# A front stage rewritten: convolution split three to one between VectorE and TensorE, softplus and u on VectorE, row clearing moved into the first expert

## The chip, the cores and the metric

The kernel runs on one core of one Trainium2 chip. The metric is the device time of one execution in microseconds, as the median of several runs; lower is better. Beside the runs there is one profiled execution, from whose trace every duration below is read.

The engines are called PE (TensorE), DVE (VectorE), ACT (ScalarE), POOL (GpSimd) and SP (SyncE, which here only issues DMAs). Each works through its own program in order and waits for others by semaphores.

## The reference, cut to what matters

The input x has 2 x 2048 tokens of 512 channels. It is normalised per token; a selective state-space layer and a mixture of eight experts both read the result.

```python
xn = layernorm(x)                                # 4096 tokens, 512 channels
# state-space branch
xc     = causal_conv4(xn, conv_w) + conv_b       # per channel, 4 taps
x_conv = silu(xc)
proj   = x_conv @ xproj_w.T                      # 128 (dt) + 16 (B) + 16 (C)
delta  = softplus(dt_in @ dtproj_w.T + dtproj_b)
a      = exp(delta * A);  b = delta * B_in * x_conv     # 16 states per channel
h      = scan(a * h + b);  s = sum(h * C_in) + xn * D_param
# expert branch: softmax over 8 experts, best 2 of a token, capacity 1024 rows an expert
scores = softmax(xn @ wg);  gate, idx = top_k(scores, 2)
pos    = cumsum(one_hot(idx)) ...                # row of the token in its expert
y      = sum(gate * (gelu(disp @ fc1_w + fc1_b) @ fc2_w + fc2_b)[idx, pos])
out    = x + s * silu(y)
```

## The kernel before

The program has two stages, `front` and `main_loop`, one behind the other with a barrier between them. `main_loop` runs eight experts; beside expert e it does the 16 scans of time chunk e. Each expert is four quarters. `front` prepares what it needs, for eight chunks of 512 tokens (`NCH` = 8, `CH` = 512), each as four blocks of 128 channels (`KT` = 4). `front` is where nearly all of the change lies.

**Normalising (L491 to L520).** Per chunk DVE measures (four `bn_stats`, `bn_aggr`, the addition of EPS), POOL copies the mean and takes the power -1/2 (L445, L447), and DVE then normalises (L512). x arrives in two buffers in turn, `got` and `s_acc` (L175); the normalised rows go to DRAM (L180). PE turns each chunk (L242) so that channels lie on partitions, ACT copies it into `xnT` (L341, L343), PE multiplies by the gate weights (L250) and ACT copies these logits twice (L349, L353). On PE the order is logits of chunk ch, turning of chunk ch+1, turning of the logits of ch.

**Routing (L564 to L614).** A chain of small dependent operations on DVE over all 4096 tokens. It needs one Exp of ACT (L368). Behind the masks PE counts with two matrices, for both choices at once (L276 to L281, into both banks of `pC`). DVE then works out the slot of each choice, and `placed` is raised when both are done. Between the counting and L288 PE waits for `placed`, since `pC` is also where it convolves.

**Convolution to softplus (L283 onwards), a loop over chunks.** Two of the four channel blocks are convolved by DVE (one `tensor_scalar` L539 and three `scalar_tensor_tensor` L543 for each), two by PE as products with diagonal matrices (L288, four taps for each block, in float32, which the trace shows as two matmuls for each product). ACT applies Silu (L376, L380). PE projects (L299, L300), turns the C rows (L316) and widens dt (L309). ACT copies the projection (L387, L390), adds the bias (L404) and does Abs, Exp and Ln (L406, L408, L415), each of Exp, Ln and Silu with a load of its table. Softplus is finished by a correction in five passes: rounding on DVE (L622), a subtraction half on POOL (L466) and half on DVE (L626), then two additions on DVE (L629, L634). POOL multiplies u = delta x_conv (L481). SP stores delta and u (L207, L212). The order on PE is `convolve(ch + 1)`, `project(ch)`, `turn_c(ch)`, `widen_dt(ch)`; DVE runs `convolve(ch + 2)` and then `soft(ch)`.

**Scatters and gathers on POOL.** The 64 scatters of the slot table (L461) are issued by POOL in pieces: 24 ahead of its work on chunk 0 and 7 ahead of that on each later chunk. When they have landed, SP loads the table (L218), DVE turns it into row numbers (L646 to L650), and POOL gathers the rows of the first expert (L474). In the last chunk these gathers stand ahead of the multiplication of u.

**Clearing y.** `dr.y` collects the experts' results by adding DMAs and must be zero first. SP clears it in `front` with five DMAs of 2 MB (L198), behind the normalised rows.

**The main loop.** SP's order in a quarter is: weights of the first matmul (L754), the B row of scan 0 (L747), weights of the second matmul, the B rows 1, 2 and 3. ACT splits each weight (L963), POOL makes its low part (L1105).

## Time and profile before

| | us |
|---|---|
| median of 3 runs | 2064.46 |
| lowest and highest | 2063.18, 2067.07 |
| the profiled execution | 2058.19 |
| its span in the trace | 2056.4 |

| engine | busy in the span |
|---|---|
| PE | 1874.2 us (91%) |
| DVE | 1825.3 us (89%) |
| POOL | 1318.3 us (64%) |
| ACT | 1227.5 us (60%) |

The profile's second part cuts the span into 40 slices of 51.4 us. PE is at a tenth of 9 from slice 7 on, and at 5 to 9 in the slices before, so a page by itself says little of `front`: the shares of the whole span are those of the main loop. To see `front` one has to cut the trace into short windows and follow single instructions. In a timeline row, the first number is the start, the second the duration of a merged group, and the bracket at the end gives the idle time of that engine ahead of it and what ended it. Granted clock 1.00 is 2.4 GHz for PE, 0.50 is 1.2 GHz.

### The profile page before, as it was taken

How to read it: one execution, taken by the hardware profiler on the slowest of the kernel's cores; microseconds unless marked ns; L12 is line 12 of the kernel's file. 1: busy time of each engine (PE TensorE's matmuls, PEld its weight loads, DVE VectorE, ACT ScalarE, POOL GpSimd, SP SyncE). 2: the span in 40 equal slices, each digit the busy share in tenths (PEclk: the TensorE clock that was granted, in tenths of full speed). 3: DMA queues.
4: the chain of work that ended last, by engine and by line, in shares of the span. 5: the costliest groups of instructions: out<-in, count | busy, mean ns of one | idle time of the engine just before them, and what ended most of it. 6: DMA issues, size and time to landing. Idle time of an engine off the chain costs nothing. (4 is left out here: it accounts for less than half of the span.)

```text
span 2056.4 us, 30191 instructions
## 1 busy us (share of the span) xinstructions
PE 1874.2 (91%) x9032; PEld 1462.8 (71%) x9032; DVE 1825.3 (89%) x1958; ACT 1227.5 (60%) x1799; POOL 1318.3 (64%) x635
## 2 busy tenths in 40 slices
PE   6599839999999999999999999999999999999940
PEld 3233227888788888888888888888888888888840
DVE  6556649989998999899989998999999998999899
ACT  3267847556655665566656575557556755665534
POOL 1167766567866686678667865786678667866530
PEclk9799979999999999999999999999999999999975
DMA  9814451124521351245114511362135212631296
GB/s 286 292 43 98 110 207 67 62 72 134 114 75 64 130 112 65 68 139 124 62 61 141 132 62 62 125 144 66 61 108 151 76 62 98 169 83 62 91 358 245
DMA packets 84867, 240.51 MB, mean 117 GB/s; under 512 B 12688, under 2 KB 13584, under 8 KB 72464
## 3 DMA queue, kind: packets, MB, share of 16 engines
q1 hardware_dynamic: 68112, 205.14, 29.2%
q0 software_dynamic: 16384, 33.63, 8.7%
q8 instruction: 66, 1.08, 0.2%
q14 instruction: 49, 0.40, 0.1%
q10 hardware_dynamic: 256, 0.26, 0.1%
HBM read 170.45 MB, written 68.55 MB: 116 GB/s over the span
## 5 line engine op out<-in xcount | busy, mean ns | idle before, releaser
L1210 DVE TENSOR_TENSOR_SCAN a_sb<-a_sb,state,ub_sb 128x512 f32<-128x512 f32 x512 | 898.4, 1795 | 12.2 <-issue 6.2
L1120 POOL TENSOR_TENSOR ub_sb<-u_sb,brow_sb 128x1024 f32<-128x1024 f32 x256 | 629.0, 2457 | 404.9 <-DVE a_sb L1210 400.4
L853 PE MATMUL pm<-xTh,w1l 128*128 128x512 f32 x1024 | 423.9, 414 | 12.9 <-POOL w1l L1105 6.2
L853 PE MATMUL pm<-w2h,hl 128*128 128x512 f32 x1024 | 422.9, 413 | 0.0
L855 PE MATMUL pm<-xTh,w1h 128*128 128x512 f32 x1024 | 402.4, 393 | 0.0
L855 PE MATMUL pm<-w2h,hh 128*128 128x512 f32 x1024 | 402.0, 393 | 0.0
L854 PE MATMUL pm<-xTl,w1h 128*128 128x512 f32 x1024 | 398.6, 389 | 0.0
L854 PE MATMUL pm<-w2l,hh 128*128 128x512 f32 x1024 | 398.6, 389 | 0.0
L1181 DVE SCALAR_TENSOR_TENSOR s_acc_keep<-pt,ct_keep,s_acc_keep 128x512 f32<-128x512 f32 x480 | 353.1, 736 | 19.8 <-PE pt L885 19.0
L1000 ACT ACTIVATE a_sb<-delta_sb,neg_a_keep 128x512 f32<-128x512 f32 x512 | 330.2, 713 | 8.0 <-DMA delta_sb<-delta_chunks 1.3
L885 PE MATMUL pt<-ident_keep,a_sb 128*128 128x128 f32 x2048 | 306.1, 272 | 3.6 <-DVE a_sb L1210 3.6
L885 PEld LDWEIGHTS pt<-ident_keep,a_sb 128*128 128x128 f32 x2048 | 252.0, 139 | 71.3 <-issue 5.5
L1023 ACT ACTIVATE hh<-pm,b_keep 128x512 fp32r<-128x512 f32 x256 | 176.0, 687 | 159.5 <-PE pm L855 155.6
L853 PEld LDWEIGHTS pm<-xTh,w1l 128*128 128x128 f32 x1024 | 193.1, 189 | 46.8 <-issue 8.8
L1105 POOL TENSOR_TENSOR w2l<-raw_keep,w2h 128x1024 fp32r<-128x1024 f32 x64 | 195.0, 3046 | 48.8 <-ACT w2h L963 48.8
L855 PEld LDWEIGHTS pm<-xTh,w1h 128*128 128x128 f32 x1024 | 192.4, 188 | 43.8
L855 PEld LDWEIGHTS pm<-w2h,hh 128*128 128x128 f32 x1024 | 192.1, 188 | 43.2
L854 PEld LDWEIGHTS pm<-xTl,w1h 128*128 128x128 f32 x1024 | 193.9, 189 | 32.5
L854 PEld LDWEIGHTS pm<-w2l,hh 128*128 128x128 f32 x1024 | 193.5, 189 | 32.6
L1198 DVE SCALAR_TENSOR_TENSOR part<-pm,gate_keep,part 128x512 f32<-128x512 f32 x256 | 187.5, 732 | 32.7 <-PE pm L855 32.7
L853 PEld LDWEIGHTS pm<-w2h,hl 128*128 128x128 f32 x1024 | 192.8, 188 | 30.8
L1190 DVE TENSOR_TENSOR hl<-pm,hh 128x512 fp32r<-128x512 f32 x256 | 174.5, 682 | 36.3 <-ACT pm L1024 32.6
(159 smaller groups left out, 1977.3 us busy)
## 6 DMA issues: line engine op xcount, KB each, us to landing
raw_keep<-in_w SPq DMA_DIRECT2D x64, 1024.0 KB, 4.8
brow_sb<-b_chunks SPq DMA_DIRECT2D x128, 256.0 KB, 3.3
moe_rows<-zeros_sb SPq DMA_DIRECT2D x5, 2048.0 KB, 16.7
xn_rows<-xn_sb SPq DMA_DIRECT2D x8, 1024.0 KB, 8.5
delta_chunks<-ln_sb SPq DMA_DIRECT2D x8, 1024.0 KB, 6.0
u_chunks<-u_now_sb SPq DMA_DIRECT2D x16, 512.0 KB, 6.0
delta_sb<-delta_chunks SPq DMA_DIRECT2D x8, 1024.0 KB, 8.3
u_sb<-u_chunks SPq DMA_DIRECT2D x16, 512.0 KB, 4.2
```

The costliest lines, as they stand in the source:

```text
L853: pe.matmul(out, sl, mh, start=start, stop=False)
L854: pe.matmul(out, sh, ml, start=False, stop=False)
L855: return pe.matmul(out, sh, mh, start=False, stop=stop)
L885: mm = pe.transpose(pt[:, bank(s, last), kt * P:(kt + 1) * P], abuf[:, m, kt, tb * P:(tb + 1) * P], ident[:])
L1000: op = act.activation(abuf[:, m, kt, :], delta[:, kt, :], ACT.Exp, scale=keep["neg_a"][:].rearrange("p n k -> p (n k)")[:, ds(col, 1)])
L1023: act.activation(hh[:, g, j, :], pm[:, j, :], ACT.Gelu, bias=bias)
L1105: op = pool.tensor_tensor(lo[:, k], w[:, k], hi[:, k].bitcast(F32), ALU.subtract)
L1120: pool.tensor_tensor(ub[:, h], u[:, 2 * h:2 * h + 2, :], brow[:, m % 2:m % 2 + 1, :].to_broadcast([P, 2, CH]), ALU.mult).then_inc(s_["bmul ...
L1181: dve.scalar_tensor_tensor(out=acc, in0=h, scalar=c, in1=acc, op0=ALU.mult, op1=ALU.add).then_inc(s_["summed"], 1)
L1190: dve.tensor_tensor(hl[:, g, j, :], pm[:, j, :], hh[:, g, j, :].bitcast(F32), ALU.subtract).then_inc(s_["h_free"], 1)
L1198: dve.scalar_tensor_tensor(out=part[:, t, :], in0=pm[:, t % 4, :], scalar=gate, in1=part[:, t, :], op0=ALU.mult, op1=ALU.add).then_inc(s_[ ...
L1210: op = dve.tensor_tensor_scan(abuf[:, m, 2 * h + k, :], abuf[:, m, 2 * h + k, :], ub[:, h, k, :], state[:, ds(col, 1)], ALU.mult, ALU.add)
```

## The change

1. **Normalising.** x has three buffers (`raw` is the third). DVE measures chunk ch+1 before it normalises chunk ch, with two sets of `stats`. POOL does the power first and the mean behind it. The first load of x stands ahead of the early constants. The final wait for all copies of `xnT` ahead of the convolution is gone, and the rows ahead of a batch are cleared at the start.
2. **Convolution.** DVE takes three of the four blocks (`VT` = 3), PE one. `conv` has two buffers, the two banks of `pC` are used in turn, and the diagonal matrices of the one block are made by POOL. Chunks 0 and 1 are convolved before the routing, and chunk 0 is projected too.
3. **Routing.** ACT does `silu(0)`, `copy_projection(0)`, `silu(1)` and `copy_ct(0)` ahead of the Exp of the routing. PE counts the first choice, waits until DVE has copied the counts out (new tile `within`, semaphore `tallied`), then counts the second in the same bank. `placed` is raised once for each choice.
4. **Softplus and u.** All five passes and the multiplication of u run on DVE. POOL has only the 64 scatters, in one piece, and the gathers.
5. **Order.** PE: `project(ch)`, `convolve(ch + 1)`, `turn_c(ch)`, `widen_dt(ch)`. ACT: `softplus(ch - 1)` stands in front of `copy_z(ch)`, with two buffers for z. DVE: `convolve(ch + 3)`, then `soft(ch)`. The table is awaited behind `soft(4)`, and SP loads it ahead of the stores of chunk 4.
6. **Clearing y.** The five DMAs leave `front`. In the first expert SP issues eight DMAs of 640 rows (1.3 MB), each behind the B row 2 or 3 of a quarter. POOL waits for them before the first adding DMA.
7. Loops of `front` are written out.

```diff
-        xin = [keep["got"], keep["s_acc"]]
+        xin = [keep["got"][:], keep["s_acc"][:], keep["raw"][:].rearrange("p (j d) -> p j d", d=D)]
+        RING = len(xin)
...
-            for r in range(0, (S + CAP) // P, 8):
-                sp.dma_start(dr.y[r * P:(r + 8) * P].rearrange("(r p) d -> p r d", p=P),
-                             zeros[:].unsqueeze(1).to_broadcast([P, 8, D])).then_inc(s_["zeroed"], 16)
-
...
+            for ch in range(NCH - 4):
                 store_du(ch)
-
             sp.wait_ge(s_["scattered"], 16 * 2 * NT)
             sp.dma_start(filled[:], dr.slots[0:TRASH].rearrange("(e p j) k -> p e j k", p=P, j=TILES)).then_inc(s_["table"], 16)
-            for ch in range(NCH - AHEAD, NCH):
+            for ch in range(NCH - 4, NCH):
                 store_du(ch)
...
             def convolve(ch):
...
+                if ch >= 2:
+                    pe.wait_ge(s_["silu"], KT * (ch - 1))
+                if ch == 3:
+                    pe.wait_ge(s_["placed"], 2)
+                for k in range(TAPS):
+                    mm = pe.matmul(pC[:, ch % 2, :], diag[:, k, :], xnT[:, ch, VT, HALO - k:HALO - k + CH],
+                                   start=(k == 0), stop=(k == TAPS - 1))
+                mm.then_inc(s_["conv_pe"], 1)
...
             convolve(0)
...
+            convolve(1)
+            project(0)
+            turn_c(0)
+            widen_dt(0)
+
+            pe.wait_ge(s_["silu"], 2 * KT)
+            for s in range(2):
+                pe.wait_ge(s_["masks"], s + 1)
+                if s == 1:
+                    pe.wait_ge(s_["tallied"], 1)
+                for k, w in enumerate((tri, ones)):
+                    mm = pe.matmul(pC[:, 1, k * NT * E:(k + 1) * NT * E], w[:], mask[s][:].rearrange("p t e -> p (t e)"), start=True, stop=True)
+                mm.then_inc(s_["counted"], 1)
+
+            for ch in range(1, NCH):
                 project(ch)
+                if ch + 1 < NCH:
+                    convolve(ch + 1)
                 turn_c(ch)
                 widen_dt(ch)
...
+            silu(0)
+            copy_projection(0)
+            store_b(0)
+            silu(1)
+            copy_ct(0)
             act.wait_ge(s_["shifted"], 1)
             act.activation(rt[1][:], rt[0][:], ACT.Exp).then_inc(s_["exped"], 1)
...
+            copy_z(0)
+            softplus(0)
+            warm_silu()
+            for ch in range(1, NCH):
                 copy_projection(ch)
-                silu(ch + 1)
+                if ch + 1 < NCH:
+                    silu(ch + 1)
                 store_b(ch)
                 copy_ct(ch)
-                softplus(ch)
...
+                if ch > 1:
+                    softplus(ch - 1)
+                copy_z(ch)
+                if ch + 1 < NCH:
+                    warm_silu()
+            softplus(NCH - 1)
...
+            measure(0)
+            for ch in range(NCH):
+                if ch + 1 < NCH:
+                    measure(ch + 1)
+                norm(ch)
...
+                for n, h in enumerate(HALVES):
+                    dve.wait_ge(s_["delta"], 2 * ch + n + 1)
+                    dve.tensor_tensor(u_now[:, h], ln[:, h], xnT[:, ch, h, HALO:], ALU.mult).then_inc(s_["u_done"], 1)
+
+            convolve(2)
+            soft(0)
+            convolve(3)
+            for ch in range(1, NCH):
+                if ch + 3 < NCH:
+                    convolve(ch + 3)
                 soft(ch)
...
+                if ch == NCH - 4:
+
+                    dve.wait_ge(s_["table"], 16)
...
+                        if begins(e):
+                            sp.wait_ge(s_["cleared"], 3)
+                            sp.dma_start(dr.y[ds((2 * q + m - 2) * ROWS, ROWS)].rearrange("(r p) d -> p r d", p=P),
+                                         zeros[:].unsqueeze(1).to_broadcast([P, ROWS // P, D])).then_inc(s_["zeroed"], 16)
...
+                pool.wait_ge(s_["zeroed"], 16 * 8)
```

## Rows read from the trace of the kernel before

**Rows 1.** Windows: per engine busy us (count), granted PE clock, DMA share, GB/s.
```profile
20.00:40.00 20.00, 16.99 (x84) 7.95 (x83) 14.19 (x40) 9.02 (x30) 3.54 (x6) 1.00 0.98 309
200.00:220.00 20.00, 18.67 (x45) 6.60 (x44) 13.88 (x16) 15.92 (x21) 15.53 (x10) 1.00 0.43 107
```

**Rows 2.** Timeline of the normalising, one chunk: start, duration, engine, line, operation, idle before.
```profile
51.63 1.92 DVE L512 TENSOR_SCALAR xn_sb<-got_keep,moments_sb,rstd_keep 128x512 f32<-128x512 f32 x4 [1.78 <-POOL rstd_keep L447]
51.78 3.60 PE L250 MATMUL pX<-xnT_sb,wg_sb 128*8 x8 [0.97 <-ACT xnT_sb L343]
53.46 2.46 DVE L494 BATCH_NORM_STATS2 stats_sb<-s_acc_keep 128x6 f32<-128x512 f32 x4
58.48 3.60 PE L250 MATMUL pX<-xnT_sb,wg_sb 128*8 128x512 f32 x8 [0.87 <-ACT xnT_sb L343]
```

**Rows 3.** Timeline of DVE and PE through the routing.
```profile
73.70 0.42 DVE L569 TENSOR_REDUCE c<-rt 128x32 f32<-128x256 f32 x1 [0.56 <-ACT rt L368]
...
84.01 0.42 DVE L594 COPY tot_sb<-pC 128x256 f32<-128x256 f32 x1 [2.18 <-PE pC L280]
...
93.99 9.34 PE L288 MATMUL pC<-xnT_sb,diag_sb 128*128 128x512 f32 x16 [10.09 <-DVEq L612]
```

**Rows 4.** Timeline of PE and ACT in the chunk loop, and ACT's same step five chunks on.
```profile
124.88 7.03 PE L288 MATMUL pC<-xnT_sb,diag_sb 128*128 x16
135.70 0.20 ACT L425 ACTIVATE f_warm<-zeros_sb 128x1 f32<-128x1 f32 x1
139.97 0.60 ACT L387 ACTIVATE dtin_sb<-pX 128x512 f32<-128x512 f32 x1 [4.07 <-PE pX L300]
141.18 0.40 PE L316 MATMUL pX<-ident_keep,bcrows_sb 32*128 32x32 f32 x4 [1.33 <-ACT bcrows_sb L390]
...
240.79 0.60 ACT L387 ACTIVATE dtin_sb<-pX 128x512 f32<-128x512 f32 x1 [4.06 <-PE pX L300]
```

**Rows 5.** Timeline of DVE: the passes of one convolution and of one softplus.
```profile
104.57 1.00 DVE L539 TENSOR_SCALAR conv_sb<-xnT_sb,chan_sb 128x512 f32<-128x512 f32 x2 [10.35 <-ACT xnT_sb L380]
105.49 4.06 DVE L543 SCALAR_TENSOR_TENSOR conv_sb<-xnT_sb,chan_sb,conv_sb 128x512 f32<-128x512 f32 x6
...
153.26 4.40 DVE L629 SCALAR_TENSOR_TENSOR back_sb<-z_sb,back_sb 128x1024 f32<-128x1024 f32 x2
...
266.89 1.29 DVE L622 TENSOR_SCALAR back_sb<-za_sb 128x1024 f32<-128x1024 f32 x2
...
273.93 2.37 DVE L634 TENSOR_TENSOR ln_sb<-ln_sb,back_sb 128x1024 f32<-128x1024 f32 x2
```

**Rows 6.** Timeline of POOL: a first, a slow, and the end of seven scatters.
```profile
226.23 0.99 POOL L461 DMA_INDIRECT slot_table<-entry_sb,place_sb  x1 [0.16 <-issue]
...
230.59 1.62 POOL L461 DMA_INDIRECT slot_table<-entry_sb,place_sb  x1 [0.30 <-issue]
...
236.08 2.35 POOL L466 TENSOR_TENSOR back_sb<-za_sb,back_sb 128x1024 f32<-128x1024 f32 x1
```

**Rows 7.** Timeline of POOL and SP: last scatter, table, last u, first DMA of the main loop.
```profile
251.86 1.05 POOL L461 DMA_INDIRECT slot_table<-entry_sb,place_sb  x1 [0.30 <-issue]
...
264.08 0.39 SPq L218 DMA_DIRECT2D filled_sb<-slot_table  x1
...
282.12 4.30 POOL L481 TENSOR_TENSOR u_now_sb<-ln_sb,xnT_sb 128x1024 f32<-128x1024 f32 x2
...
292.72 0.34 SPq L737 DMA_DIRECT2D d_row<-in_D  x1
```

**Rows 8.** DMA issues of the page: KB each, median us from issue to landing.
```profile
raw_keep<-in_w SPq DMA_DIRECT2D x64, 1024.0 KB, 4.8
delta_chunks<-ln_sb SPq DMA_DIRECT2D x8, 1024.0 KB, 6.0
```

**Rows 9.** Timeline of SP and ACT in the first expert: a weight's load and its use.
```profile
370.73 0.34 SPq L754 DMA_DIRECT2D raw_keep<-in_w  x1
...
379.30 1.92 ACT L963 ACTIVATE w1h<-raw_keep 128x2048 fp32r<-128x2048 f32 x1
```

More of the change, by code:

```diff
@@ new lines, in copy_ct, with copy_z @@
+            def copy_ct(ch):
+                act.wait_ge(s_["ct"], ch + 1)
+                apart(act, s_["act_at"])
+                act.activation(keep["ct"][:, TPC * ch:TPC * (ch + 1), :], pX[:, 1, 0:TPC * 2 * N].rearrange("p (j n) -> p j n", n=2 * N)[:, :, N:], ACT.Copy).then_inc(s_["ct_copied"], 1)
+            def copy_z(ch):
+                if ch >= 2:
+                    act.wait_ge(s_["soft"], 2 * (ch - 1))
+                for kt in range(KT):
+                    act.wait_ge(s_["dt"], KT * ch + kt + 1)
+                    act.activation(z[:, ch % 2, kt, :], pT[:, kt, :], ACT.Identity, bias=chan[:, kt, C_DTB:C_DTB + 1]).then_inc(s_["dt_read"], 1)
@@ new lines, in power @@
+                pool.tensor_copy(keep["mean"][:, ch, :], moments[:, ch % 2, :, 0]).then_inc(s_["power"], 1)
+            for ch in range(NCH):
+                power(ch)
+            pool.wait_ge(s_["consts"], 16 * len(consts))
+            for k in range(TAPS):
+                op = pool.tensor_scalar(diag[:, k, :], ident[:], chan[:, VT, C_TAP + HALO - k:C_TAP + HALO - k + 1], None, ALU.mult)
+            op.then_inc(s_["diag"], 1)
+            pool.wait_ge(s_["defaults"], 16)
+            for s in range(2):
+                pool.wait_ge(s_["placed"], s + 1)
+                apart(pool, s_["pool_at"])
+                for t in range(NT):
@@ new lines, in norm @@
+            def norm(ch):
+                u, v = ch % RING, ch % 2
+                dve.wait_ge(s_["power"], 2 * ch + 1)
+                if ch >= 2:
+                    dve.wait_ge(s_[f"xn_out{v}"], 16 * (ch // 2))
+                    dve.wait_ge(s_["xT"], KT * (ch - 1))
+                for j in range(TPC):
+                    op = dve.tensor_scalar(xn[:, v, j, :], xin[u][:, j, :], moments[:, v, j, 0:1], keep["rstd"][:, ch, j:j + 1],
+                                           ALU.subtract, ALU.mult)
+                op.then_inc(s_["normed"], 1)
@@ L547, in _ @@
             convolve(0)
[L548 to L552 removed]
+            convolve(1)
             chain = [0]
@@ L633, in soft @@
+                for n, h in enumerate(HALVES):
+                    dve.wait_ge(s_["dropped"], 2 * ch + n + 1)
+                    dve.scalar_tensor_tensor(out=back[:, h], in0=zc[:, h], scalar=0.0, in1=back[:, h], op0=ALU.max, op1=ALU.add).then_inc(s_["soft"], 1)
+                for n, h in enumerate(HALVES):
+                    dve.wait_ge(s_["soft"], 2 * ch + n + 1)
                     dve.wait_ge(s_["lnz"], 2 * ch + n + 1)
                     dve.tensor_tensor(ln[:, h], ln[:, h], back[:, h], ALU.add).then_inc(s_["delta"], 1)
-            for ch in range(1, AHEAD):
-                convolve(ch)
@@ L638, in _ @@
-            with dve.Fori(0, NCH - AHEAD) as ch:
-                convolve(ch + AHEAD)
-                soft(ch)
-            for ch in range(NCH - AHEAD, NCH - 1):
-                soft(ch)
-            dve.wait_ge(s_["table"], 16)
-            dve.tensor_copy(keep["add_row"][:, 0], vacant[:, 0, :, 0])
-            dve.tensor_copy(keep["add_row"][:, 1:], filled[:, :, :, 0])
-            dve.tensor_copy(keep["gate"][:], filled[:, :, :, 1])
-            dve.tensor_scalar(keep["row"][:, E], vacant[:, 0, :, 0], float(S - 1), None, ALU.min)
@@ L650, in _ @@
-            dve.tensor_scalar(keep["row"][:, 0:E], filled[:, :, :, 0], float(S - 1), None, ALU.min).then_inc(s_["indexed"], 1)
-            soft(NCH - 1)
+                if ch > 0:
+                    dve.wait_ge(s_["u_out"], 32 * ch)
+                for n, h in enumerate(HALVES):
+                    dve.wait_ge(s_["delta"], 2 * ch + n + 1)
+                    dve.tensor_tensor(u_now[:, h], ln[:, h], xnT[:, ch, h, HALO:], ALU.mult).then_inc(s_["u_done"], 1)
+            convolve(2)
+            soft(0)
```

419 lines of the change are left out of this document (179 added, 240 removed).

## The prediction, made before the changed kernel ran

> **What bounds the kernel now.** I read the windows of the first 320 us first, then the timeline of each engine in them, and the waits last. `front` ends at 292.7 us, where SP issues the first DMA of the main loop [rows 7]; the rest, 1763.7 us of the span, the change touches only in the first expert. So the question is when SP gets to that row.
>
> `front` has three parts. While x is normalised, DMA is 98% busy at 309 GB/s and no engine is full [rows 1]. The matmuls of the logits start 6.70 us apart, 3.60 us of work with PE waiting for ACT's copies in front [rows 2]: a circle of PE and ACT. DVE's circle has the same length, with 1.78 us of waiting for POOL. Then comes the routing, a chain on DVE with PE idle: PE's convolution of chunk 0 starts at 93.99, behind a wait for DVE [rows 3]. Last is the chunk loop. There PE is busy 18.67 of 20 us, ACT 15.92, POOL 15.53, DVE 13.88 [rows 1]; ACT waits 4.07 us in each round for PE's projection, and five rounds take 240.79 - 139.97 = 100.8 us, 20.16 each [rows 4]. PE is the bound. Behind the last round stand softplus, the gathers and u on POOL until 286.42, and 6.3 us more until 292.72 [rows 7], for the last store to land and the barrier.
>
> **Part 1, normalising: about 0 (-1.5 to +1.5).** Measuring one chunk ahead takes POOL's 1.78 us out of DVE's circle, not out of that of PE and ACT, which keeps 6.7 to 6.9 us a chunk; DMA, at 98%, would not allow much less either. The first normalisation now stands behind a second measuring (2.46 us of statistics and some 0.6 us of small steps [rows 2]) but without the wait for POOL: 1 us later. At the end the logits are ready at about 71, and nothing of a convolution lies between them and the routing if DVE has its two convolutions done by then; if not, the next part hides it. POOL's four diagonal products have no row: a DVE pass costs 1.0 us for two of four times the width [rows 5], so 0.3 to 1 us each, while POOL is idle anyway: nothing.
>
> **Part 2, routing: later by about 17 us.** PE convolves chunks 0 and 1 (3.45 us each, half of the 6.9 us between the start of a convolution and of the next step [rows 4]) and projects chunk 0. The projection takes 139.97 - 124.88 - 6.9 = 8.2 us [rows 4]. From 71: 71 + 6.9 + 8.2 = 86.1. ACT then does two copies (1.0), four Silu (2.1), the C rows (0.2), a table load and the Exp (1.7): 91.3. Before, the Exp was done at 73.70 [rows 3]. DVE has nothing to do in between, since all its other work stands behind the routing in its program. From 73.70 to the wait of 2.18 us ahead of 84.01 are 8.1 us; the wait for the counts is gone, as PE counts the first choice beside the chain. Both rounds took 84.01 to about 93.9 = 9.9 us [rows 3]; two more pairs of copies add 0.9, the last product 0.3. DVE is free at 91.3 + 8.1 + 9.9 + 0.9 + 0.3 = 110.5; the first choice is placed at 104.6. What is bought with the 17 us: PE and ACT have chunk 0 behind them, and ACT its softplus.
>
> **Part 3, the chunk loop: a shorter round, with DVE as its bound.** PE's round loses half of its convolution and, with the other half set between the projection and the C rows, the wait of 1.33 us for ACT's copy [rows 4]: 20.16 - 3.45 - 1.33 = 15.4 us. ACT's round is the same work; from the warm-up's end at 135.90 it waits until 139.97, and nowhere else, so its work is 20.16 - 4.07 = 16.1 us [rows 4]. DVE's round grows. Convolution: three `tensor_scalar` at 0.46 and nine further passes at 0.66 = 7.35 [rows 5]. Softplus: rounding 1.3, the subtraction on both halves 2.5 (taken as two-input passes of 1.2, with the semaphore step), the two additions 2.4 each [rows 5]. u has no row on DVE; its nearest is the two-input pass of L634, 2.37 for two, and the bound above is POOL's 4.30 for the same [rows 7]. I take 2.4. Softplus with u is 11.0, the round 18.35 us, above 15.4 and 16.1. What DVE no longer meets is POOL's elementwise work, beside which two additions took 4.40 us in place of 2.4 [rows 5].
>
> From 110.6 DVE has six convolutions and five softpluses to the end of `soft(4)`: 44.1 + 55.0 = 99.1, which is 209.7, if nothing holds it.
>
> **Part 4, the table.** POOL scatters from 104.6 on. Seven scatters took 236.08 - 226.23 = 9.85 us, 1.41 each, one of them 1.62 with 0.30 between [rows 6]. All between 0.99 and 1.62, with the gap, gives 1.29 and 1.92 as bounds; I take 1.46, a little above the group, as DVE is fuller than it was: 64 x 1.46 = 93.4, to 198.0. SP loaded the table 11.2 us after the last scatter had been issued (264.08 - 252.91 [rows 7]); why so late no row says, and I keep it: 209.2, landed 2.7 us later. DVE waits 2 us and goes on at 212.4. The stores of chunk 4 stand behind this load on SP, and ACT's Ln of chunk 5 behind that store (6.0 us [rows 8]).
>
> A rule bears on this part. The row shows scatters of 1.62 us among others of 0.99 [rows 6]. The Trainium skill, SBUF - State Buffer, section "Who interferes with whom", says that a `tensor_scalar` of VectorE in a two-port mode locks GpSimd out of a shared port for its whole length, and that descriptors can't be written meanwhile. By that rule the 2.7 us of such passes in a round of 18.35 would be lost to POOL, which gives 1.49 us a scatter, 2 us more on the whole than my 1.46.
>
> **Part 5, the tail.** Without convolutions DVE needs 11 us for a chunk and ACT 16, so ACT leads. Ln of chunk 5 is done at about 219, DVE ends chunk 5 at 223.3. ACT then has the bias, warm-up, the copies, Abs, table and the first Exp of chunk 6: 228.8; DVE waits 5.5 us and ends at 240.2. In chunk 7 Ln waits for delta of chunk 6 to be stored (237.8 + 6.3 = 244.1) and DVE ends with u at 251.3. The gathers (8, taken like the scatters at 1.3 to 1.9 us each, from 212 on) are hidden now. With the same 6.3 us [rows 7]: 257.6. `front` is shorter by 292.7 - 257.6 = 35.1 us.
>
> **Part 6, clearing y: about +1 (0 to 34).** Taken out of `front` it gives nothing, as nothing waited for it. In the first expert a clear of 1.31 MB is at 309 GB/s [rows 1] 4.2 us of DMA, ahead of a B row or of a weight. A weight was issued at 370.73 and used at 379.30, 8.6 us later, and needs 4.8 to land [rows 8, 9]; with a clear in front some 8 to 9. It fits with nothing to spare, and behind ACT's split there is more slack for PE. I take 1 us for all eight.
>
> **Sum.** -35.1 + 1 = -34 us. On the profiled execution (2058.2 us, span 2056.4, 6.3 below the median of the runs) that is 2024; on the median 2064.5 - 34 = 2030.5 us.
>
> **The rivals.**
> - *The tail costs nothing, and the loop is DVE's alone.* 110.6 + 132.1 + 0.5 + 6.3 = 249.5: -43 + 1, 2022 us. For it: Ln waits only where stores take 6 us, and smaller DMA load may shorten them. Against it: ACT's 16.1 against DVE's 11 in three chunks. 0.15.
> - *The scatters are late.* DVE is now full, and each scatter may meet one of its passes. At the slow row's 1.62 + 0.30 = 1.92 us for all [rows 6] they end at 227.4; `front` would end near 287, which gives 2060. At 1.6 it ends near 267 and gives 2040. For it: single slow rows. Against it: in a group of seven at most four are slow. 0.21, mostly near 1.6. By the lock rule of the Trainium skill (SBUF - State Buffer, "Who interferes with whom") it would stay near 1.5, as said.
> - *Nothing is gained.* The 35 us would go if DVE's seven rounds were 5 us longer each: passes of 2.7 us at double length, or u on DVE at POOL's 4.30 us with waits between dependent passes. Nothing on POOL can stretch them so now. 2064 us; 0.04.
> - *Slower: the clears hold back the first expert.* Each stands on SP's queue ahead of the next B row and weight. If the main loop, with PE full there, stops by more than (34 + 1 + 4)/8 = 4.9 us for each, the kernel is slower than before beyond the measurement; at 5.5 us it is 2064.5 - 35 + 44 = 2073. Against it: the slack of 3.8 us at the weight [rows 8, 9] absorbs nearly all of 4.2. 0.05.
>
> **How the numbers follow.** Forecast 0.55 (2025 to 2036, the bounds of part 1, of the store and of the scatters up to 1.55), then the rivals above. Faster by over 0.2% (4.1 us, about what a measurement of this kernel can tell from no change): 0.55 + 0.15 + 0.20 = 0.90; within 0.05 (the third and the edge of the second); slower 0.05. The range goes from 2020, which takes in most of the first rival, to 2044, which takes in scatters of 1.6; about 0.17 is left out.
>
> **What would show it.** The Exp of the routing ends near 91 and the last `placed` near 110; PE's matmuls of a round fill 15.4 us and leave gaps; DVE's rounds are 18.3 us with no gap from chunk 2 to 4; POOL shows scatters alone, the last one issued near 198; the table is loaded near 209; u of chunk 7 ends near 251, SP starts the main loop near 258; ACT's weight splits of the first expert have no wait in front. Wrong would be: an Exp far from 91, a round of DVE over 20 us, a table behind 215, or weight splits that wait for a DMA.

## The result: 17 us faster, half of the forecast

| | before | changed |
|---|---|---|
| median of the runs | 2065.46 us | 2048.33 us |
| lowest and highest of the changed kernel | | 2037.07, 2055.63 |
| ratio, with its 95% interval | | 0.9917 (0.989 to 0.9945) |
| the profiled execution | 2058.19 us | 2037.07 us |
| its span | 2056.4 us | 2035.3 us |
| the main loop begins at | 292.7 us | 275.8 us |
| from there to the end of the span | 1763.7 us | 1759.5 us |

The median of before is here that of five runs; the forecast was made from the first three of them, 2064.46 us. The kernel is faster, but by 17 us and not by 34, and the time lies above the range. The profiled execution of the changed kernel is the fastest of its five. One run of the kernel before, of 3966.22 us in the second round of experiments, was in a slow state and is left out of the ratios. By its own sum `front` should have ended at 257.6; it ended at 275.8, 18.2 us late. The main loop was some 5 us better than the forecast of +1. Together that is 13 us of the 18 that are missing; the other 5 are the distance of the profiled execution to the median, 11.3 us here and 6.3 before.

The page of the changed kernel, its first part and its clearing DMAs:

```profile
PE 1859.4 (91%) x8968; PEld 1453.9 (71%) x8968; DVE 1854.6 (91%) x2009; ACT 1225.0 (60%) x1790; POOL 1292.3 (63%) x615
...
moe_rows<-zeros SPq DMA_DIRECT2D x8, 1280.0 KB, 6.4
```

VectorE is now as busy as TensorE, GpSimd a little less than before. The timelines say more. First the routing, the lines that answer to [rows 3]: start, length, engine and line, names, and in brackets the idle time ahead with what ended it.

```profile
90.00 0.42 DVE L531 TENSOR_REDUCE c<-rt 128x32 f32<-128x256 f32 x1 [19.17 <-ACT rt L398]
...
110.13 1.58 DVE L505 TENSOR_SCALAR conv_sb<-xnT_sb,chan_sb 128x512 f32<-128x512 f32 x3
```

```profile
104.57 1.25 POOL L439 DMA_INDIRECT slot_table<-entry_sb,place_sb  x1 [48.14 <-DVEq L576]
...
136.68 14.85 POOL L439 DMA_INDIRECT slot_table<-entry_sb,place_sb  x1 [0.30 <-issue]
```

The routing came as forecast: the Exp ends at 89.97, VectorE has waited 19.17 us for it, the first scatter goes out at 104.57 and the convolutions go on at 110.13. But then one scatter of GpSimd, an instruction of which most last about 1 us here, lasts 14.85 us. The lines that answer to [rows 5] and [rows 7], VectorE beside it and later, and SP:

```profile
136.63 6.05 DVE L508 SCALAR_TENSOR_TENSOR conv_sb<-xnT_sb,chan_sb,conv_sb 128x512 f32<-128x512 f32 x9
...
143.79 2.36 DVE L589 TENSOR_TENSOR back_sb<-za_sb,back_sb 128x1024 f32<-128x1024 f32 x2
...
154.62 2.36 DVE L601 TENSOR_TENSOR u_now_sb<-ln_sb,xnT_sb 128x1024 f32<-128x1024 f32 x2 [3.92 <-DMA u_chunks<-u_now_sb]
...
188.54 0.69 DVE L586 TENSOR_SCALAR back_sb<-za_sb 128x1024 f32<-128x1024 f32 x1 [5.19 <-issue]
...
223.23 2.36 DVE L601 TENSOR_TENSOR u_now_sb<-ln_sb,xnT_sb 128x1024 f32<-128x1024 f32 x2 [8.43 <-DMA u_chunks<-u_now_sb]
234.72 0.17 DVE L613 CAST add_row_keep<-vacant_sb 128x8 int32<-128x8 f32 x1 [9.13 <-DMA filled_sb<-slot_table]
```

```profile
164.12 9.04 POOL L439 DMA_INDIRECT slot_table<-entry_sb,place_sb  x1 [0.30 <-issue]
...
221.13 0.96 POOL L439 DMA_INDIRECT slot_table<-entry_sb,place_sb  x1 [0.30 <-issue]
```

```profile
232.48 0.38 SPq L200 DMA_DIRECT2D filled_sb<-slot_table  x1
...
275.78 0.34 SPq L704 DMA_DIRECT2D d_row<-in_D  x1
```

The passes have about the lengths that were forecast. Between them VectorE waits: for the stores of u (3.92, 1.33 and 8.43 us), once at a pass that needs ScalarE's Exp (5.19, which the profile puts to no releaser), and for the table (9.13). The Exp was late because ScalarE had stood for 7.52 us, until 178.85, ahead of its copy of a projection that TensorE had finished at 170.6; what held it there no row shows. SP could load the table only at 232.48, 10.4 us behind the last scatter, which was itself issued at 221 and not at 198. The groups of waits from 104 to 276 us show the same for the two others: ScalarE's Ln waits for the store of delta, its copy of the B rows for the store of B.

```profile
L439 POOL DMA_INDIRECT slot_table<-entry_sb,place_sb x64 | 98.3, 1536 | 67.3 <-DVEq L576 48.1 <-issue 19.2
...
L390 ACT ACTIVATE ln_sb<-za_sb 128x1024 f32<-128x1024 f32 x14 | 14.0, 1050 | 13.1 <-DMA delta_chunks<-ln_sb 11.7 <-issue 1.4
...
L358 ACT ACTIVATE bcrows_sb<-pX 32x512 f32<-32x512 f32 x7 | 4.0, 578 | 10.9 <-DMA b_chunks<-bcrows_sb 10.9
```

The 64 scatters cost 98.3 us of GpSimd, 1536 ns each on average, 1.84 us with the gap of 0.30, where 1.46 with the gap was forecast. Alone (e1 below) they cost 61.9. Of the 36 us between, two scatters of 14.85 and 9.04 us make up 22. Two questions follow: why do scatters take so long, and why do the stores land so late?

### The profile page after: what moved, and what is told of

It is laid out like the page before. It is cut to its first block and busy times, and to the rows that moved or that the text cites. A ratio compares the mean times of both kernels' runs of the same rounds, so it can differ in the third digit from the quotient of the medians.

```text
span 2035.3 us, 29262 instructions
## 1 busy us (share of the span) xinstructions
PE 1859.4 (91%) x8968; PEld 1453.9 (71%) x8968; DVE 1854.6 (91%) x2009; ACT 1225.0 (60%) x1790; POOL 1292.3 (63%) x615
```

## The experiments

Theories at the start. **A**: the DMA engines take 2.0 us for each scatter, one behind the other, and stores queue behind them. **B**: the scatters and the large stores hold each other up in the DMA engines. **C**: VectorE's passes keep GpSimd from issuing. The time of the kernel before on the chips of these three rounds was 2062.8, 2068.1 and 2062.8 us (medians of seven).

### Scatters alone, and nearly none

e1 awaits the table right behind the routing, with neither a store nor a pass of VectorE beside the scatters.

```diff
-            for ch in range(NCH - 4):
-                store_du(ch)
             sp.wait_ge(s_["scattered"], 16 * 2 * NT)
...
+            dve.wait_ge(s_["table"], 16)
...
             convolve(2)
```

> The changed kernel with one thing moved: DVE waits for the slot table right behind the routing, before its convolution of chunk 2, and SP loads the table ahead of all stores of delta and u. So the 64 scatters run with nothing else on DVE and no large store beside them. Theory A (each scatter of 128 eight-byte writes takes about 2.0 us to complete, one behind the other, whatever stands beside it): SP's load of the table comes 120 to 135 us after the first scatter is issued, though POOL could issue all in about 82. Theory B (the scatters are late because of the large stores beside them): about 83 to 95 us. Theory C (DVE's passes keep POOL from issuing): the same 83 to 95 us, with scatters of 0.96 us each and none longer. The time of the kernel by A is about 2037 + 110 = 2150, by B and C about 2110.

Measured: 2100.05 us. The group of the scatters, then SP's load, the last scatter and one gather of the same run, issued when VectorE was at its chunks:

```profile
L437 POOL DMA_INDIRECT slot_table<-entry_sb,place_sb x64 | 61.9, 967 | 71.9 <-DVEq L574 52.8 <-issue 19.2
```

```profile
200.23 0.36 SPq L198 DMA_DIRECT2D filled_sb<-slot_table  x1
```

```profile
187.74 0.96 POOL L437 DMA_INDIRECT slot_table<-entry_sb,place_sb  x1 [0.30 <-issue]
...
282.14 27.38 POOL L444 DMA_INDIRECT s_acc_keep<-xn_rows,row_keep  x1 [0.30 <-issue]
```

Alone, a scatter takes 967 ns and none is long. The table is loaded 92.6 us after the first of them, not 128, so A is refuted. The lag of 11.5 us between the last scatter and the load stays, with nothing beside it. And the gathers, the same kind of instruction on GpSimd, took up to 27.38 us each once VectorE had its passes back. A single run gave this time.

e2 issues 2 of the 64 scatters; the rows of nearly all tokens are then those of vacant slots.

```diff
-                for t in range(NT):
+                for t in range(1):
...
-            sp.wait_ge(s_["scattered"], 16 * 2 * NT)
+            sp.wait_ge(s_["scattered"], 16 * 2)
```

> The changed kernel with 2 of its 64 scatters (the first of each choice); the other 62 are left out, so that nearly all slots stay vacant and the gathered rows are not those of the reference. Theories A, B and C alike: DVE's waits for stored u (3.9, 1.3 and 8.4 us), for the table (9.1) and ACT's for stored B rows and delta go, and the main loop starts at 248 to 254 in place of 275.8, near the 249.5 that DVE's work alone gives. Time 2012 to 2018, and the spread of the runs (2037 to 2056 of the changed kernel) shrinks to about 3 us. If the main loop still starts later than 262, the scatters are not what held the front. That all gathers now fetch one row may add something in the main loop, which its own length will show.

Measured: 2005.95 us (2005.35 to 2008.29), ratio 0.9726 (0.9709 to 0.9744).

```profile
167.70 0.33 SPq L191 DMA_DIRECT2D delta_chunks<-ln_sb  x1
...
185.32 0.33 SPq L191 DMA_DIRECT2D delta_chunks<-ln_sb  x1
...
245.42 0.34 SPq L704 DMA_DIRECT2D d_row<-in_D  x1
```

The stores of delta are 17.62 us apart, which is VectorE's round, and the main loop starts at 245.42. That is earlier than expected (248 to 254), and the time is 6 us below its range. So the scatters cost `front` some 30 us in the changed kernel, and without them something close to the first rival of the prediction (main loop at 249.5) is what happens. One gather of this run, at 205.83, again lasts 10.87 us, with no scatter near it.

### Wider rows, and two buffers

e3 makes the rows of the slot table 64 bytes instead of 8 (`W` is 16 words of 4 bytes). It asks whether the narrow rows are what makes the lag behind the last scatter and the stores long.

```diff
-        self.slots = dram("slot_table", (E * CAP + 2 * S, 2))
+        self.slots = dram("slot_table", (E * CAP + 2 * S, W))
...
-        entry = sb("entry_sb", [P, 2, NT, 2])
+        entry = sb("entry_sb", [P, 2, NT, W])
```

> The changed kernel with slot rows of 64 bytes in place of 8 (14 more words of zeros in each entry; same 64 scatters, same 8192 descriptors, eight times the bytes; the table is loaded whole, 512 KB). [...] Theory A2 (the cost is one of each descriptor or of each scatter, whatever its bytes): table near 232 as before, time within 5 us of the changed kernel. Theory B (large stores): as A2.

Measured: 2041.89 us (2035.02 to 2042.67), ratio 0.9886 (0.9862 to 0.991). The scatters in it, and VectorE beside the first long one:

```profile
120.23 11.31 POOL L444 DMA_INDIRECT slot_table<-entry_sb,place_sb  x1 [0.31 <-issue]
...
140.21 16.40 POOL L444 DMA_INDIRECT slot_table<-entry_sb,place_sb  x1 [0.30 <-issue]
...
180.74 11.30 POOL L444 DMA_INDIRECT slot_table<-entry_sb,place_sb  x1 [0.30 <-issue]
...
234.33 0.96 POOL L444 DMA_INDIRECT slot_table<-entry_sb,place_sb  x1 [0.30 <-issue]
```

```profile
120.33 1.28 DVE L593 TENSOR_SCALAR back_sb<-za_sb 128x1024 f32<-128x1024 f32 x2
121.54 2.35 DVE L596 TENSOR_TENSOR back_sb<-za_sb,back_sb 128x1024 f32<-128x1024 f32 x2
...
128.35 2.35 DVE L608 TENSOR_TENSOR u_now_sb<-ln_sb,xnT_sb 128x1024 f32<-128x1024 f32 x2
130.62 1.59 DVE L512 TENSOR_SCALAR conv_sb<-xnT_sb,chan_sb 128x512 f32<-128x512 f32 x3
```

SP's load of the table, and VectorE's wait for it:

```profile
236.44 0.38 SPq L203 DMA_DIRECT2D filled_sb<-slot_table  x1
```

```profile
240.96 0.17 DVE L621 CAST add_row_keep<-vacant_sb 128x8 int32<-128x8 f32 x1 [31.94 <-DMA filled_sb<-slot_table]
```

The busy time by stretch in this run (columns: stretch, its length, the busy time of PE, PEld, DVE, ACT and POOL with their instructions, granted clock, DMA share, GB/s):

```profile
120.00:128.00 8.00, 6.55 (x14) 1.30 (x12) 8.00 (x9) 4.23 (x9) 7.77 (x1) 1.00 0.03 6
128.00:136.00 8.00, 8.00 (x22) 3.19 (x22) 8.00 (x12) 1.07 (x2) 6.78 (x5) 1.00 0.68 265
```

This run separates three things. The lag behind the last scatter is 1.2 us (235.29 to 236.44) instead of 10 to 11. The stores now move at 265 GB/s with a DMA share of 0.68, and VectorE waits for none of them; in the changed kernel the DMA engines were busy with far less to show for it (below, at e9). But GpSimd still stands for 39 us in three scatters. From 120 to 128 the DMA share is 0.03: the DMA engines were nearly idle while the scatter stood. It begins 0.1 us ahead of VectorE's softplus and ends 0.8 us behind its last pass. B is refuted for the scatters, and C is left. VectorE, held up by no store, reaches the table sooner and waits 31.94 us for it; in the profiled run the main loop starts at 282.00, later than in the changed kernel. The median is 6.4 us lower, and the two intervals overlap: by itself the edit gives nothing clear.

e4 has two buffers each for delta, u and the B rows, with rows of 8 bytes, and loads the table two chunks later.

```diff
-                    act.wait_ge(s_["delta_out"], 16 * ch)
+                    act.wait_ge(s_[f"delta_out{ch % 2}"], 16 * (ch // 2))
...
-            for ch in range(NCH - 4):
+            for ch in range(NCH - 2):
                 store_du(ch)
```

> The changed kernel with two buffers for delta, u and the B and C rows, used in turn (so a store may take a whole round longer before anybody waits for it), and the table awaited behind soft(6) in place of soft(4), with SP's load of it behind the stores of chunk 5. The scatters are as they were. Theory A: completions stay late, but nobody waits for them except for the table at about 232, which DVE reaches at about 226 to 232; the main loop starts at 250 to 256, time 2013 to 2020. If completions of the stores weren't what ACT and DVE lost time to, it starts where it did, near 270.

Measured: 2043.39 us (2034.44 to 2044.29), ratio 0.9893 (0.9863 to 0.9922).

```profile
L444 POOL DMA_INDIRECT slot_table<-entry_sb,place_sb x64 | 117.2, 1832 | 67.5 <-DVEq L581 48.4 <-issue 19.2
```

Expected were 2013 to 2020 us if late stores were the loss; that missed. Nothing waits for a store but one Ln (4.9 us); the scatters are worse (1832 ns), the last one ends at 240.82, and VectorE waits 23.5 us for the table. Waiting for stores is therefore not what makes the scatters late. In both e3 and e4, three scatters of 11.3, 16.4 and 11.3 us stood at the same places of VectorE's round.

### VectorE's passes: a gap, or a wait, between them

In the changed kernel a pass waits for the one two places back, so the passes run into one another, 1.135 us apart where one alone takes 1.23. e5 puts a short memset and a wait for it ahead of each stage of softplus and u and ahead of three taps.

```diff
+            def gap():
+                gaps[0] += 1
+                dve.memset(tiny[:, 0:1], 0.0).then_inc(s_["gap"], 1)
+                dve.wait_ge(s_["gap"], gaps[0])
...
+                gap()
                 for n, h in enumerate(HALVES):
                     dve.wait_ge(s_["rounded"], 2 * ch + n + 1)
```

> The changed kernel with a short memset of one column and a wait for it, on VectorE, ahead of each of the five stages of a chunk's softplus and u and ahead of taps 1 to 3 of its convolution (8 places a chunk, from chunk 2 of the convolution on); nothing else differs. Theory C (VectorE's passes, issued one right behind the other, keep GpSimd from finishing the descriptors of a scatter; the scatters of 11.3, 14.9 and 16.4 us all begin at the start of such a stretch and end 0.9 us after its last pass): a scatter now gets in at a gap, so none lasts over 4 us and the last of the 64 ends at about 195 to 205 instead of 222; the table loads some 11 us behind it (206 to 216 instead of 232.5); the gaps cost VectorE 0.15 to 0.25 us each, 64 in all, 10 to 16 us; VectorE is then the bound or the stores are: main loop at 258 to 270, median 2018 to 2035 against 2041 to 2048. Theory B (a scatter waits while the large stores hold the DMA engines): scatters of 9 to 16 us stay, two or three of them, the last ends at 220 or later, and the time rises by the gaps, 2048 to 2060.

Measured: 2030.54 us (2029.43 to 2035.04), ratio 0.9821 (0.9789 to 0.9853).

```profile
L440 POOL DMA_INDIRECT slot_table<-entry_sb,place_sb x64 | 72.1, 1127 | 69.8 <-DVEq L586 50.6 <-issue 19.2
...
L518 DVE MEMSET tiny_sb<- 128x1 f32 x58 | 3.4, 59 | 18.5 <-DMA u_chunks<-u_now_sb 10.6 <-issue 7.9
```

```profile
125.56 1.99 POOL L440 DMA_INDIRECT slot_table<-entry_sb,place_sb  x1 [0.30 <-issue]
...
197.37 1.17 POOL L440 DMA_INDIRECT slot_table<-entry_sb,place_sb  x1 [0.31 <-issue]
```

```profile
213.51 1.47 SPq L196 DMA_DIRECT2D u_chunks<-u_now_sb  x2
215.03 0.46 SPq L201 DMA_DIRECT2D filled_sb<-slot_table  x1
...
274.27 0.34 SPq L719 DMA_DIRECT2D d_row<-in_D  x1
```

No scatter lasts over 1.99 us, and the last ends at 198.5, 23.6 us earlier. The only thing added is 58 memsets of 0.06 us on VectorE, each with a wait. That is C, shown by an intervention: what VectorE does makes the scatters long. The second half of the expectation missed: the main loop starts at 274.27 in the profiled run, not at 258 to 270. The memsets are where VectorE now waits 18.5 us; 10.6 of it the profile puts to stores of u, and for the other 7.9 the program has no other wait there. SP's load of the table stands behind such a store (213.51). With the scatters in time, the slow stores became the bound. The median is 17.8 us below the changed kernel's, though the profiled run, the slowest of four here and the fastest of five there, starts the main loop only 1.5 us earlier.

e6 adds no instruction but waits: each pass waits for the one directly ahead. One of the six places:

```diff
-                    dve.wait_ge(s_["dropped"], 2 * ch + n + 1)
+                    dve.wait_ge(s_["dropped"], 2 * ch + 2)
+                    dve.wait_ge(s_["soft"], 2 * ch + n)
```

> The changed kernel with each pass of VectorE in the chunks' convolution, softplus and u waiting for the pass directly ahead of it (as the kernel before did in its softplus: passes 1.26 us apart instead of 1.135), no other instruction added. Theory C with any gap being enough (the wait leaves 0.03 us between two passes): no scatter over 4 us. Theory C with the gap too short to be used: scatters of 9 to 16 us stay. Either way VectorE's round of 17.6 us becomes about 19.5 us (10 passes x 0.1 and 12 x 0.07).

Measured: 2042.95 us in a single run; scatters of 1111 ns on average, none over 1.67 us, the last ending at 195.0. A few hundredths of a microsecond between two passes are enough. VectorE again waits for stores of u (7.5 and 9.6 us), the table is loaded only at 218.96, behind a store on SP's queue, and the main loop starts at 281.79.

The traces of all runs fall on two sides. The six whose passes run into one another (the changed kernel, e1 to e4, e8) each have a scatter or a gather of over 10 us; the seven with gaps or waits (e5 to e7, e9 to e12) have none over 2.1 us.

### Both causes together

e7 takes the gaps, the rows of 64 bytes, two buffers and the table two chunks later; e8 is the same without the gaps.

> Four edits together: the gaps of the run e5, slot rows of 64 bytes, two buffers each for delta, u and the B rows, and the table loaded and used behind chunk 6's softplus. Theory C plus the collision of 8-byte scatters with the stores (these took 8 to 14 us to land beside 8-byte scatters at a DMA share above 0.8 and under 130 GB/s, while with 64-byte rows the same stores ran at 265 GB/s): no scatter over 4 us, last one ends at 195 to 210, table loads 1 to 2 us behind the last or behind its queue place, no wait for a store over 3 us, VectorE the only bound with 10 to 16 us of gaps on it: main loop starts at 252 to 262, median 2012 to 2025. Without theory C: the scatters end at 235 or later and the main loop starts at 275 or later, 2035 to 2050.

> The same as the run e7 but without the gaps: 64-byte slot rows, two buffers, table behind chunk 6. Theory C: scatters of 11 to 16 us stay (about 39 us over their 1.3 us each), last one ends at 235 to 242, the table loads right behind it, main loop starts at 270 to 282, median 2030 to 2045; against e7 the difference is the price of the long scatters less that of the gaps. If instead the lag behind the last scatter and the slow stores were all that cost: 2006 to 2015, and the gaps only add to it.

Measured: e7 2023.95 us (2022.41 to 2025.03), ratio 0.979 (0.9757 to 0.9822); e8 2030.6 us (2025.9 to 2035.22), 0.9815 (0.978 to 0.9851). Both medians lie in their ranges; the two intervals overlap. In e8 the three long scatters are back and the last ends at 243.9. In e7 the scatters end at 204.3 and VectorE at 249.56, but the main loop starts later than its 252 to 262:

```profile
250.69 0.95 POOL L457 DMA_INDIRECT s_acc_keep<-xn_rows,row_keep  x1 [0.30 <-issue]
```

```profile
248.51 1.62 SPq L200 DMA_DIRECT2D u_chunks<-xn_sb  x2
263.40 0.34 SPq L734 DMA_DIRECT2D d_row<-in_D  x1
```

The main loop begins 11.8 us behind the last gather, and 13.3 us behind the last store, where 4 to 5 us are the rule (e2: 245.42 - 241.11 = 4.3). In e8 it was 11.4 us behind the last gather. The late table had moved the gathers to the end, where they show a lag of their own; its cause is open.

e9 therefore keeps the table at the place of the change and has only the gaps and the wide rows. Its table is loaded into the memory of `entry`, whence the name in the row.

> Two edits on the changed kernel: the gaps of e5 and the 64-byte slot rows of e3; single buffers and the table's place as in the change. If the two found causes (scatters starved by VectorE's passes; stores slowed by 8-byte scatters) add up and nothing else is there: scatters end at 200 to 205, table loaded at 203 to 208, no wait of VectorE over 2 us in the chunks, last u ends at 249 to 252, main loop at 254 to 257, median 2010 to 2016. The gathers of e7 ended at 251.6 and its main loop began 11.8 us later, though the last store had been issued at 250.1; if that lag belongs to the gathers, here it is gone, as they are issued by 235. If it belongs to something else, the main loop starts at 260 to 266 as in e7 and the median is 2018 to 2025.

Measured: 2014.0 us (2013.08 to 2016.81), ratio 0.9763 (0.9734 to 0.9792).

```profile
202.95 0.38 SPq L204 DMA_DIRECT2D entry_sb<-slot_table  x1
...
253.28 0.34 SPq L727 DMA_DIRECT2D d_row<-in_D  x1
```

```profile
152.00:168.00 16.00, 16.00 (x41) 5.42 (x41) 15.64 (x28) 15.92 (x23) 12.83 (x11) 1.00 0.38 141
```

```profile
152.00:168.00 16.00, 12.47 (x24) 4.41 (x24) 13.38 (x19) 11.79 (x16) 13.26 (x10) 0.69 0.92 115
```

All terms came as expected or less than 1 us sooner (the scatters end at 201.78). The gaps cost VectorE 18.94 - 17.62 = 1.3 us a round (its stores of delta here against e2), 0.17 us for each of the eight. The last two fences are the same stretch in e9 and in the changed kernel: 0.38 of the DMA engines for 141 GB/s against 0.92 for 115. Beside the gaps the wide rows are worth 2030.5 - 2014.0 = 16.5 us (e5 to e9), beside the wide rows the gaps 27.9 us (e3 to e9). Alone against the changed kernel's 2048.3 they gave 6.4 and 17.8 us, together 34.3, by medians from several chips. By the ratios, each taken to the kernel before of its own round, the gain over the changed kernel is 0.3% and 1.0% alone and 1.5% together, each known to about 0.4%, so the size of what the two do to each other is not clear of the noise. That each hides a part of the other the traces show: without the long scatters VectorE waits for stores (18.5 us in e5), without the slow stores for the table (31.94 us in e3), and without either for nothing longer than 2.1 us (e9).

e10 adds two buffers to e9.

> As e9 with two buffers each for delta, u and the B rows. If the stores land in time with 64-byte rows, two buffers bring nothing: the same as e9 within 2 us. If the stores still hold VectorE or ScalarE in e9, this one is 3 to 10 us faster.

Measured: 2012.82 us (2012.32 to 2014.44), ratio 0.9756 (0.9728 to 0.9784): the same as e9 within 1.2 us. With stores that land in time, a second buffer is worth next to nothing.

### The 19 us of waiting for the Exp

e11 is e9 with ScalarE's Exp of the routing ahead of `silu(0)` and TensorE's counts ahead of `convolve(1)`.

```diff
+            act.wait_ge(s_["shifted"], 1)
+            act.activation(rt[1][:], rt[0][:], ACT.Exp).then_inc(s_["exped"], 1)
             silu(0)
...
-            convolve(1)
             project(0)
             turn_c(0)
             widen_dt(0)
...
                 mm.then_inc(s_["counted"], 1)
+            convolve(1)
```

> As e9, and the routing's Exp is put back ahead of ScalarE's silu of chunk 0, with TensorE's counts ahead of its convolution of chunk 1: in the changed kernel VectorE waits 19.2 us for this Exp. The Exp should run at 71 to 73 instead of 89.6, the routing end at 91 to 94 instead of 110, and all that VectorE does after it come 15 to 19 us earlier if VectorE is the bound, main loop at 236 to 242, median 1992 to 1999. If ScalarE or TensorE is late with chunks 0 and 1 (silu of chunk 1 now waits for counts and softplus of chunk 0), part of it is lost: 2000 to 2008.

> As e11 with two buffers and, instead of the gaps, the waits of e6 (each of VectorE's passes waits for the one directly ahead). In e6 they too kept every scatter under 2 us; their price is about 0.1 us a pass against 0.11 us a gap with 8 gaps a chunk and 22 passes a chunk, so 0 to 1 us a chunk more: main loop 0 to 8 us later than in e11, 1992 to 2005. If waits of 0.03 us don't always let GpSimd in, a scatter of 9 us or more is back and the table comes later, which chunks behind it cover or not: up to 2015.

Measured: e11 2003.25 us (2003.08 to 2005.78), ratio 0.9706 (0.9679 to 0.9734); e12 2014.05 us (2012.96 to 2015.36), 0.976 (0.9731 to 0.9788).

```profile
88.99 0.42 DVE L571 COPY tot_sb<-pC 128x256 f32<-128x256 f32 x1 [8.37 <-PE pC L301]
```

```profile
244.54 0.34 SPq L725 DMA_DIRECT2D d_row<-in_D  x1
```

The Exp now starts at 71.84, but of the 17.8 us that VectorE waited for it in e9, 8.37 came back as a wait for the counts, which stand on TensorE behind the projection and the widened dt of chunk 0. The main loop starts 8.7 us earlier than in e9, short of the 236 to 242 of the first expectation, and the time is 10.7 us less, as in its second. It is the fastest of the kernels with all scatters, 2.9% under the kernel before. e12 had no long scatter either (1150 ns on average), but it is 10.8 us slower than e11 and above the 2005 expected without a long scatter: its waits cost VectorE more than the gaps do: its stores of delta are 20.4 us apart against 18.94 in e9 and e11 and 17.62 with neither (e2). The expectation of at most 1 us a chunk between them was too low by a third of what was measured (1.5). That the second buffers of e12 gave nothing back is likely from e10, not shown by itself.

## Why the prediction was wrong

**Held.** Part 1: the logits were ready at 69.97 (71 forecast). Part 2: Exp at 89.97 (91.3), first scatter out at 104.57 (104.6), convolutions at 110.13 (110.5). Part 3: VectorE is the bound and its round is 17.67 us where it is not held up, from 7.33 for a convolution and 10.34 for a softplus with u (18.35 forecast, since the passes ran into one another); e2 had it at 17.62. Of the signs of being wrong, two came: a table behind 215 (232.48) and rounds over 20 us (the stores of delta at 150.78 and 172.42 are 21.64 apart). u on VectorE costs 2.35 us (2.4). Part 6: the eight clears did not slow the first expert, no weight split of it waits for a DMA; the main loop's stretch was 4.2 us shorter than before, against the +1 of the forecast, and why is open.

**Failed: part 4, the duration of a scatter.** The term was 64 x 1.46 us, taken from seven scatters of before [rows 6], with bounds of 1.29 and 1.92 us. The mean was 1.84. The second rival had priced this: by its sum 1.84 a scatter starts the main loop near 281 (275.8 measured). But the rival got a chance of 0.21, "mostly near 1.6", and lay outside the range at 1.84. The mistake was in what the row was read for. Those scatters stood beside a VectorE that was busy 13.88 us in 20 [rows 1] and whose passes had waits between them; the change fills VectorE and lets its passes follow without a break, from 110.13 to 150.69 at one stretch. Beside the convolution's passes a scatter mostly takes 1.0 to 1.5 us still (but one gather of e1, from 221.97 to 229.45, stood beside nothing else). Beside those of softplus it takes either 1.96 us, which with the gap of 0.30 is two passes of 1.135, or it gets in nowhere and stands until that run of softplus passes is over (0.8 to 0.9 us behind its last pass, in the changed kernel and in e3). Three of the five long ones in these two began 0.1 us ahead of a softplus, the other two already beside the convolution ahead of it. What decides between 1.96 us and the long stand, the moment at which it starts or the kind of pass, no run separates. That a fuller VectorE might hurt was in the text, as a single pass met by a scatter; that a scatter may stand through a whole run of passes was in no row of before, where none of the 64 lasted over 1.67 us.

The rule that was weighed beside it was the wrong half of the page. The Trainium skill, SBUF - State Buffer, section "Who interferes with whom", also states that a VectorE instruction with two SBUF inputs contends with a GpSimd instruction that reads SBUF. The scatter's offsets (`place_sb`) lie there. The long scatters lie over such passes (four of softplus' five stages read two of them), so the trace doesn't contradict this rule, but it doesn't show it either: three of the convolution's four taps also read two, and beside them most scatters took 1.02 us, while the first stage of softplus, two `tensor_scalar`, reads one and let no long scatter through (there the rule weighed in the prediction might hold it). By the prediction's working that rule gave 1.49 us a scatter; 1.84 was measured. The section infers besides that the writing of descriptors is not touched by `tensor_tensor`; these scatters speak against taking that for an indirect DMA as a whole.

**Failed: parts 3 to 5, the stores.** They were priced at the 6.0 us of [rows 8], and for VectorE at nothing ("209.7, if nothing holds it"). u of chunk 0 was issued by 128.54 and VectorE waited for it until 154.62, 26 us later. The rows of 64 bytes remove this (e3, e9). So 8-byte scatters beside the stores make them slow; why they did so less before, where 8-byte scatters ran too and a median store landed in 6.0 us, is not settled. One difference is that before, GpSimd issued them in groups of seven with its own work between. In the changed kernel these waits ended before the table came, so they cost nothing on top of it; in e5 and e6 they are the bound.

**Held, its cause left open: the lag in part 4.** The 11.2 us behind the last scatter were kept, rightly (10.4). It goes with the 8-byte rows (1.2 us in e3, e8 and e9).

**How they join.** The scatters end at 222.1 and not at 198.0; with the lag the table is loaded at 232.5, 23 us late. VectorE, held up 13.7 us by stores of u and 5.4 us at ScalarE's Exp, ends chunk 4 at 225.6, waits 9.1 us for the table and goes on at 234.7, 22.3 us behind the forecast of 212.4. The tail gives 4.1 of them back (41.1 us to the main loop, 45.2 forecast), 1.4 of that in the last store (270.91 to 275.78, 4.9 and not 6.3). That leaves the 18.2 us.

A kernel whose scatters hit or miss VectorE's boundaries should also vary from run to run. The five runs of the changed kernel span 18.6 us, those of e3, e4 and e8 7.7 to 9.9 us, those without long scatters (e2, e5, e7, e9 to e12) 2.1 to 5.6 us. But the kernel before, whose trace has no long scatter, spread over 6.1 to 10.5 us in its three sets of seven (without the run of 3966.22), so this shows nothing by itself.

**Not tried**: the same kernel with its delta and u never stored, before with its passes run together, and gaps beside softplus or beside the convolution alone.

## What to carry to other kernels

When work is moved to an engine that will then be full, look at which other engine needs its pauses, not only its time: GpSimd's indirect DMAs stood still for whole runs of softplus passes on VectorE, and a break of 0.17 us in eight places of a chunk brought the last scatter 24 us forward. Price a small operation by the rows whose surroundings match those after the change, not by the nearest rows of the kernel before. And when a fix of one cause brings little, look for the second one behind it: in the profiled runs the gaps brought the main loop 1.5 us forward, the wide rows put it 6.2 us back, both together brought it 22.5 us forward. Single profiled runs vary, so take the medians beside them: there the gaps alone gave 17.8 us and the wide rows 6.4.

## What the runs showed of the hardware

- An indirect DMA on GpSimd, 0.96 to 1.2 us alone, took mostly 1.02 us beside the convolution's passes of VectorE (0.66 us apart). Beside those of softplus (1.135 us apart) it took 1.96 us in step with two of them, or stood still for 9 to 27 us (9.04 in the changed kernel, 27.38 in e1) until such a run of passes was over. Once, in e1, one stood for 7.48 us beside passes of the convolution alone.
- A memset of 0.06 us with its wait between VectorE's stages, or only the wait for the pass ahead, was enough to let it in: none lasted over 2.1 us in e5 to e7 and e9 to e12.
- Rows of 8 bytes against 64: the lag from the last scatter to a load that waits for it alone was 9.1 to 11.5 us against 1.2, and in the same stretch the DMA share was 0.92 at 115 GB/s against 0.38 at 141. Behind the last of the gathers (rows of 2 KB) such a lag of 9.2 to 11.8 us showed with either (e4, e7, e8).
- TensorE's clock: in the changed kernel it fell to the lower of its two levels behind a wait, and the same eight products took 6.61 us instead of 3.70. The first row is of a round with a wait of 1.24 us, the last stands behind one of 6.84. In the window the granted clock is 0.50, which is 1.2 GHz.

```profile
132.58 3.70 PE L282 MATMUL pT<-dtin_sb,dtprojT_sb 128*128 128x512 f32 x8
...
155.53 0.60 PE L274 MATMUL pX<-ident_keep,bcrows_sb 32*128 32x32 f32 x4 [6.84 <-ACT bcrows_sb L358]
156.06 6.61 PE L282 MATMUL pT<-dtin_sb,dtprojT_sb 128*128 128x512 f32 x8
```

```profile
152.00:160.00 8.00, 4.47 (x9) 2.35 (x10) 5.38 (x8) 5.18 (x9) 6.32 (x6) 0.50 1.11 160
```

It cost nothing by itself here: TensorE was busy 4.47 us in these 8, and it had finished the next projection (170.6) before ScalarE was ready for it (171.32). The DMA share of 1.11 in this row can't be a busy share; beside 8-byte rows the column serves only to compare one window with another.
